# Sliding-window attention in a five-stage kernel: the exponential taken head by head out of PSUM with a negative-maximum bias

## The reference, cut to what matters

```python
qkv = jnp.einsum('bsi,oi->bso', x, w_qkv)
q, k, v = heads(q), heads(k), heads(v)          # (b, 16, s, 8)
scores = jnp.einsum('bhqd,bhkd->bhqk', q, k) / jnp.sqrt(8)
allowed = (j <= i) & (i - j < WINDOW)
scores = jnp.where(allowed, scores, -jnp.inf)
attn = jax.nn.softmax(scores, axis=-1)
ctx = jnp.einsum('bhqk,bhkd->bhqd', attn, v)
return jnp.einsum('bso,po->bsp', ctx, w_out) + b_out
```

## Time and profile before

| | us |
|---|---|
| median of 3 runs | 563.32 |
| lowest, highest run | 561.24, 566.46 |
| profiled execution, its own time | 567.4 |
| its span | 565.7 |
| PE busy | 478.8 (85%) |
| DVE busy | 441.8 (78%) |
| ACT busy | 269.4 (48%) |
| POOL busy | 311.8 (55%) |

### The profile page before, as it was taken

The page is one execution under the profiler, slowest core; times in us unless marked ns, Lnnn a source line. Parts: engine busy times, 40 slices in busy tenths (PEclk is TensorE's granted clock), DMA queues, the critical chain, the costliest instruction groups (busy, mean ns, idle before and its releaser), DMA issues.

```text
span 565.7 us, 10087 instructions
## 1 busy us (share of the span) xinstructions
PE 478.8 (85%) x3866; PEld 293.2 (52%) x3866; DVE 441.8 (78%) x884; ACT 269.4 (48%) x417; POOL 311.8 (55%) x232
## 2 busy tenths in 40 slices
PE   3999988999999999999588689787688778687995
PEld 2676777787776767776232234233233323245664
DVE  4578778676769566667965999999899989998753
ACT  1426665555556523656784637343343334320742
POOL 3158301202100011567301998999999999994574
PEclk9999999989899889999985798989989979999998
DMA  7000000000000000000019544354553345100011
GB/s 214 2 0 2 5 1 2 3 2 3 2 2 3 2 0 2 2 0 2 0 28 390 232 206 156 122 223 159 213 222 148 149 166 224 56 2 0 2 37 38
DMA packets 12322, 42.74 MB, mean 76 GB/s; under 512 B 2857, under 2 KB 8754, under 8 KB 10226
## 3 DMA queue, kind: packets, MB, share of 16 engines
q1 hardware_dynamic: 11458, 41.56, 19.2%
q10 hardware_dynamic: 816, 0.53, 0.3%
HBM read 40.78 MB, written 1.31 MB: 74 GB/s over the span
## 4 chain that ended last, share of the span: by engine, by line
PE 41%; DVE 22%; issue 16%; POOL 12%; ACT 6%; DMA 1%; POOLq 0%; ACTq 0%; DVEq 0%
DVE hst L1030 7%; PE bk L441 6%; PE bk L447 6%; PE bk L704 5%; PE bk L690 5%; POOL hC L1101 4%; PE bk L677 3%; DVE xnT L278 3%; PE bk L1172 3%; POOL dBu L1084 3%; DVE dBu L1009 2%; PE bk L665 2%; ACT g L836 2%; PE bk L1120 2%; POOL powers L292 2%
## 5 line engine op out<-in xcount | busy, mean ns | idle before, releaser
L1101 POOL TENSOR_TENSOR hC<-hst,rows 128x1024 f32<-128x1024 f32 x63 | 147.2, 2382 | 3.6 <-DVE hst L1030 3.6
L1030 DVE TENSOR_TENSOR_SCAN hst<-bk,dBu 128x1024 f32<-128x1024 f32 x64 | 144.3, 2275 | 4.5 <-POOL dBu L1084 4.5
L1172 PE MATMUL bk<-hC,ident 128*128 128x512 f32 x256 | 126.7, 629 | 2.8 <-ACT ysb L1251 1.6
L1261 ACT ACTIVATE bk<-delta,aneg 128x1024 f32<-128x1024 f32 x64 | 71.5, 1118 | 108.2 <-DVE hst L1030 108.0
L285 POOL TENSOR_TENSOR veps<-mv,lneps 128x4 f32<-128x4 f32 x24 | 5.7, 239 | 165.4 <-DVE mv L257 165.3
L1172 PEld LDWEIGHTS bk<-hC,ident 128*128 128x128 f32 x256 | 50.7, 201 | 55.9 <-issue 45.0
L514 ACT ACTIVATE rows<-bk 128x512 f32<-128x512 f32 x64 | 38.1, 597 | 63.9 <-PE bk L441 63.9
L1152 PE MATMUL bk<-s,sel 96*128 96x512 bf16 x96 | 32.4, 422 | 38.2 <-DVE dBu L1009 38.1
L560 DVE TENSOR_REDUCE smax<-bk 128x4 f32<-128x512 f32 x64 | 43.6, 682 | 24.6 <-PE bk L677 24.6
L1009 DVE TENSOR_TENSOR dBu<-bk,du 128x1024 f32<-128x1024 f32 x48 | 57.6, 1201 | 6.3 <-PE bk L1152 5.3
L836 ACT COPY g<-bk 128x512 f32<-128x512 f32 x64 | 37.4, 584 | 48.5 <-PE bk L690 47.9
(11 more groups left out here) (172 smaller groups left out, 757.6 us busy)
## 6 DMA issues: line engine op xcount, KB each, us to landing
rows<-c_rows SPq DMA_DIRECT2D x16, 2048.0 KB, 7.1
rows<-c_rows SPq DMA_DIRECT2D x4, 1024.0 KB, 9.6
x<-in_x_dram SPq DMA_DIRECT2D x4, 256.0 KB, 5.0
out_dram<-x SPq DMA_DIRECT2D x4, 256.0 KB, 2.3
wmoe<-in_w_dram ACTq DMA_DIRECT2D x2, 256.0 KB, 5.6
wup<-in_upT_dram SPq DMA_DIRECT2D x1, 256.0 KB
wdn<-in_downT_dram SPq DMA_DIRECT2D x1, 256.0 KB
wproj<-in_in_wT_dram SPq DMA_DIRECT2D x1, 256.0 KB
```

Source lines behind the costliest of these rows:

```text
L1030: nc.vector.tensor_tensor_scan(hst[k % 3][:, :], dA[k % 2][:, :], dBu[k % 3][:, :], 0.0, ALU.mult, ALU.add).then_inc(m2["scan"], 1)
L1101: nc.gpsimd.tensor_tensor(hC[k % 4][:, :], hst[k % 3][:, :], crep[:, k % 12, :], ALU.mult).then_inc(m2["hC"], 1)
L1172: last = nc.tensor.matmul(bk01[:, r * CH:(r + 1) * CH], ident[:, :], hC[k % 4][:, r * CH:(r + 1) * CH], start=(k % NS == 0), stop=(k % NS ...
L1261: nc.scalar.activation(dA[k % 2][:, :], delta[:, i, :], ACT.Exp, scale=aneg[:, h * NS + n:h * NS + n + 1]).then_inc(m2["dA"], 1)
```

## The change

DVE no longer subtracts. It negates the four maxima of a block into a small tile `nmax` (128x4), and ACT computes the exponential of each head straight from the bank of scores in PSUM, with that head's column of `nmax` as the instruction's per-partition bias. So a block has four ACT instructions of 128x128 where it had one of 128x512, and the bank is free only once ACT has read it: `mask_scores` and `expert_up` wait for the exponentials (`at["p"]`) and no longer for DVE (`at["sub"]`). The wait on the transposes of the tile before goes from DVE to ACT, which now writes `ssub` first; DVE waits for the previous tile's exponentials before it writes `nmax`.

```diff
+        nmax = sb("nmax", [P, H])
@@ attn_vector, soften
                 dve.wait_ge(at["max"], t * JG + j + 1)
-                m = smax[:, j * HPG:(j + 1) * HPG].rearrange("p (a o) -> p a o", o=1).to_broadcast([P, HPG, P])
                 if t > 0:
-                    dve.wait_ge(at["pt"], t * JG - JG + j + 1)
-                nc.vector.tensor_tensor(ssub[:, j, :].rearrange("p (a k) -> p a k", a=HPG), s3d, m,
-                                        ALU.subtract).then_inc(at["sub"], 1)
+                    dve.wait_ge(at["p"], t * JG - JG + j + 1)
+                nc.vector.tensor_scalar(nmax[:, j * HPG:(j + 1) * HPG], smax[:, j * HPG:(j + 1) * HPG], -1.0, None,
+                                        ALU.mult).then_inc(at["sub"], 1)
@@ attn_tensor, mask_scores
                 if t > 0:
-                    pe.wait_ge(at["sub"], t * JG - JG + j + 1)
+                    pe.wait_ge(at["p"], t * JG - JG + j + 1)
@@ attn_tensor, expert_up
-                pe.wait_ge(at["sub"], NT * JG - JG + k + 1)
+                pe.wait_ge(at["p"], NT * JG - JG + k + 1)
@@ attn_scalar, probs
                 act.wait_ge(at["sub"], t * JG + j + 1)
-                nc.scalar.activation(ssub[:, j, :], ssub[:, j, :], ACT.Exp).then_inc(at["p"], 1)
+                if t > 0:
+                    act.wait_ge(at["pt"], t * JG - JG + j + 1)
+                for a in range(HPG):
+                    h = j * HPG + a
+                    last = nc.scalar.activation(ssub[:, j, a * P:(a + 1) * P], bank[j][:, a * P:(a + 1) * P], ACT.Exp,
+                                                bias=nmax[:, h:h + 1])
+                last.then_inc(at["p"], 1)
```

## The result

The changed kernel takes 583.04 us (median of 4 runs, 581.77 to 586.38) against 564.8 us for the kernel before (median of 4, the three shown above and one more beside it). The ratio is 1.0326, with a 95% interval from 1.0276 to 1.0377: slower by 18 us. The profiled execution took 582.51 us, with a span of 580.8, where the one of before had 567.4 and 565.7; between these two the difference is 15.1 us. Executions over 1.5% above the fastest of the same kernel are left out of every ratio in this document; two of one_exp (among them its profiled one, 570.95 us), two of no_bias and two of the kernel before are such.

What follows compares the result with a forecast made beforehand. With ACT's queue closing a loop with PE in the attention, 1.7 + 5 x 1.31 + 3 x (0.6 + 0.2 + 1.0) + 0.6 = 14.2, taken as +15 us: 563.3 + 15 = 578.5 us, range 571 to 587.

Steps and rivals of the forecast that it cites:

- the first tile: Interval from tile 0's scores to the next tile's: 8.75 us forecast against 7.04 before, +1.7.
- the tiles with t mod 4 = 1: Three attention tiles that also project the next chunk: intervals of 9.8 us against 9.23, +0.6 each.
- behind the last scores: Stretch after the attention's last scores, where PE has expert matmuls to fill in: +0.6 us.
- ACT's queue in a loop with PE: Next scores wait for the last exponential: 3.06 us through PE plus ACT's copies 1.60 and exponentials 4.47, 9.13 us.
- The plain tile: Tiles without projections, five intervals: 9.13 us between starts of scores against 7.82, +1.31 each.
- ACT's price: Four 128x128 exponentials with bias, 0.383 us each, 0.273 apart: ACT held 1.09 us a block against 0.54 before.
- signs of being right: Attention: exponentials 0.37 to 0.39 us, 0.26 to 0.29 apart; plain tiles 9.0 to 9.4; ACT over 120 us; DVE down some 33.
- DVE's cover: DVE is early throughout a plain tile: maximum and nmax end 2.1 us after scores start, first exponential can start at 3.27.
- The bound of one microsecond in a tile: Small nmax multiplications waiting for GpSimd: 0 to +1 us in each of four tiles, 0 to +4 in all.
- The clock: Rival: PE's share at 1.2 GHz in the attention grows from a tenth to two, +5 us, 584; chance 0.11.
- The late release: Bank of scores free only after the exponential, so block 3's mask in the next tile waits for this tile's last exponential.
- The break-even of 0.76 us for a block: Rival, not slower: loop 4.77 + 4B meets 7.82 us when a block holds ACT B = 0.76; chance 0.09.

Runs made afterwards that it cites:

- one_exp: Changed kernel with one maximum per block over its four heads, so one 128x512 exponential with bias replaces four: 0.9984 of the kernel before.
- no_bias: Changed kernel with its four 128x128 exponentials but without the bias operand, the maximum left out of the exponent: 1.0022 of the kernel before.
- dve_double: Changed kernel with DVE's subtraction put back as idle work, written to a tile nobody reads: 1.0323 of the kernel before.
- neg_reduce: Changed kernel with the maximum negated inside the reduction, so the 64 small multiplications are gone: 1.026 of the kernel before.
- repetition: The changed kernel run once more, unaltered, as yardstick for two other runs: 1.0305 of the kernel before.
- wait_only: Kernel before, with only the masks' and expert matmuls' wait moved from DVE's subtraction to the exponential: 1.0009 of the kernel before.
- split_only: Kernel before, each 128x512 exponential split into four of 128x128, still after DVE's subtraction, without bias, old bank release: 1.0065 of the kernel before.
- early_after: Changed kernel with the transposes of block 3 moved directly behind the next tile's scores, ahead of values 0 and 1: 1.0049 of the kernel before.

## Why the prediction was right

**The sum.** The forecast for the profiled execution was 582.4 us, and it took 582.51; the forecast for the median was 578.5, and it was 583.04, inside the range. The 15 us were right for the two profiled executions. The medians differ by 3 us more (18.2), since the profiled execution of before lay 2.6 us above the median of its four runs, and that of the changed kernel 0.5 below its own. That the profiled time was met to 0.1 us is luck: by the table the sum was 1.4 us short on the first tile and 1.4 on the tiles with t mod 4 = 1, and 1.6 over behind the last scores, and of the 15 us almost one was allowed for things not worked out. The cause, ACT's queue in a loop with PE, is not luck; the chain of tile 4 and the experiments show it.

**The plain tile.** 9.13 us was forecast, 9.12 measured, though some of its terms were off and cancelled. The exponentials start 0.254 us apart, not 0.273, so eight of them until the copy took 2.01 and not 2.18, and four until the next copy 1.02 and not 1.09. The last four took 1.28 to their result in tile 4 and not 1.20, and the way back through PE, from there to the scores' start, 0.44 (100.22 to 100.66) and not 0.27: half of the pair's 0.43 in the earlier trace rows is the pace of masks in a row, while a mask that is waited for takes 0.39, as the row of 100.27 shows. A term read from a row in a stream is too small for an instruction that stands behind a wait.

**ACT's price.** Four exponentials held ACT 1.02 us, forecast 1.09. The Trainium skill, "ScalarE: Activation LUTs", section "What ACT_TABLE_LOAD costs", has a 128x512 with a pointer bias at 280 + 0.833 x 512 = 707 ns, an estimate by its rule; the trace of one_exp agrees with 702. For 128x128 its 387 ns is under the 404 ns median, and its overlap of 93 ns is under the 150 ns seen here (404 less 254). By these two figures four would hold ACT 1.18 us, an estimate; the measured 1.02 decides. Three of the prediction's signs of being right were missed here: single exponentials took 404 ns and not 370 to 390, they start 0.254 apart and not 0.26 or more, and ACT was busy 114 us in the stage and not over 120.

**ACT's and DVE's busy time.** ACT's rose by 28.9 us in the program, where 16 x 4 x 0.55 = 35 us would follow from the prediction's terms of 1.09 and 0.54 us for a block. DVE's fell by 27.4 us, not by some 33: the subtractions were 44.2 us, but the multiplications took 16.1 and not 10.9, with a mean of 251 ns over a median of 170.

**DVE's cover.** The 64 subtractions brought next to nothing, as the prediction's loop demanded; dve_double shows that directly.

**The first tile** was mis-sized: +3.1 for +1.7. The small multiplications, costed at 0.17 us and hidden, ran beside GpSimd's selections there. The timeline of tile 0, and the source view of L565 (min/median/max in ns):

```profile
49.98 4.16 POOL L1391 TENSOR_SCALAR_AFFINE_SELECT sel<-sel 96x2048 bf16<-96x2048 bf16 x2
...
52.64 1.52 DVE L565 TENSOR_SCALAR nmax<-smax 128x4 f32<-128x4 f32 x1
...
54.28 2.00 POOL L1433 TENSOR_SCALAR_AFFINE_SELECT sel<-sel 96x2048 bf16<-96x2048 bf16 x1
54.78 1.52 DVE L565 TENSOR_SCALAR nmax<-smax 128x4 f32<-128x4 f32 x1
...
56.34 1.14 ACT L834 ACTIVATE g<-bk,nmax 128x128 f32<-128x128 f32 x4 [0.53 <-DVE nmax L565]
```

```profile
L565 DVE TENSOR_SCALAR nmax<-smax x64: 170/170/1524, 51.5 to 204.1; 128x4 f32<-128x4 f32 x64
```

Two of them took 1.52 us, one of them ended with GpSimd's pair of selections and the other with the third, and exponentials 2 waited 0.53 us. The Trainium skill's rule of the exclusive lock ("SBUF — State Buffer", section "SBUF: two separate sides"), stated there for a DVE operation in a two-port mode, has the one that comes second wait for the other's whole instruction. The trace agrees, with the two ends of 54.16 and 56.30 against the selections' 54.14 and 56.28; in which mode the multiplication ran it does not show. The bound of one microsecond in a tile was too narrow for that place; neg_reduce's first tile of 8.53 against a forecast of 8.75, which counted a multiplication, confirms the rest of the term. The median of 170 ns was right for the other tiles.

**Tiles with t mod 4 = 1** took 3.2 us more in sum, forecast 1.8, and those with 3 took 2.5 more, forecast 3.0. Both sums hold stretches at 1.2 GHz: 10.88, 10.04 and 11.06 are the long ones of the changed kernel, 9.92 and 9.67 of before. Without such stretches (a granted clock of 1.00 over the interval, in the changed kernel or its repetition) the tiles took 9.64 to 9.79, 9.92 and 9.89 for t mod 4 = 1, 2, 3: the first 0.0 to 0.2 below the forecast, the others 0.1 to 0.2 above.

**The clock** was named as a rival with a chance of 0.11 and a granted clock under 0.90; it was 0.91 and 0.92 in two profiles of the changed kernel, against 0.95. What it did can be read off the intervals. Against tiles of the same kind at the upper clock, the ones with a stretch at 1.2 GHz were longer by 1.2, 0.7 and 1.0 us (tiles 7, 8, 11) in the kernel before, 2.9 in all, and by 1.1, 1.2, 0.4, 0.2, 0.3 and 0.4 (tiles 1, 3, 5, 8, 12, 14) in the changed one, 3.5 in all. Tile 0 is left out of this; the changed kernel's was granted 0.89 and took 10.10 us, dve_double's 1.00 and 9.86. So the lower clock accounts for about one of the 16 us by which the intervals grew. A plain tile that waits for ACT hides most of it: 0.15 to 0.4 us here, 0.74 before. dve_double had 0.95 and was as slow, one_exp 0.90 and no_bias 0.91 and were not. The mention that 450 to 500 us showed no such effect was no evidence for the attention.

**The late release,** taken in the prediction as part of the loop, costs nothing that can be measured in the whole by itself (wait_only), and the splitting little (split_only, 3.7 us). It is the bias's 0.09 us in each of 256 instructions, with the splitting and inside the loop, that makes 18 us. The break-even of 0.76 us for a block fits: no_bias at 0.65 and one_exp at about 0.6 (an estimate, 0.702 less the overlap of 0.11) are level, the changed kernel at 1.02 is not. No run lies between 0.65 and 1.02, so the point itself is not shown.

## What to carry to other kernels

Before work is moved from a busy engine to an idle one, follow the idle one's queue through a whole round: an engine that is busy half of the program and 70% of the stage (114 of 163 us) can set the pace once the producer waits for its last instruction. Count per-instruction costs there, four small instructions with a per-partition operand against one large, and look for a form that keeps one, such as a shift common to four heads, which took the 3% back (0.9984). When a loop of two engines sets the pace, take out of it what it doesn't need, by an order of the in-order queues; here four transposes moved ahead of the values took 16 us from the changed kernel and 7 from the one before, on which no change of operations alone gained anything that can be measured.

## What was not expected of the hardware

A per-partition bias costs 0.09 us of ACT's time in each instruction even where neighbours overlap (0.254 against 0.163 us apart), and four times that is 0.37 us a block. Four instructions of 128x128 without it hold ACT only 0.65 us out of PSUM (0.80 out of SBUF), against some 0.54 for one of 128x512 out of SBUF.

PE's clock did not follow its busy share. In the stage it was granted 0.95 in the kernel before with PE busy 151 of 163 us, 0.92 with only the later release (151 us), 0.91 without the bias (150 us) and 0.90 with one exponential per block (153 us), 0.91 and 0.92 in the changed kernel (145 and 144 us), 0.94 in neg_reduce (145 us), 0.95 in dve_double (142 us) and 0.97 with only the splitting (149 us). In all four kernels with the transposes of block 3 moved up it was 0.98, with PE busy 142 us (early_after) or 151 to 152 us. PE's work per tile is the same in all of these, but a faster kernel has more of what follows the attention in the window, and each figure is one execution; whole executions of the kernel before alone spread from 0.918 to 0.955. The move goes with a high clock, and isn't the only way to one (split_only). What of it keeps the clock up was not settled.

DVE's small operation from SBUF to SBUF was held up to 1.52 us beside a GpSimd selection, for 0.17 us of work.
